# Wider instructions and another order in the pass towards the states

## The reference

```
fx = layer_norm(x, ln1_g, ln1_b)
lam_bar = exp(lam * dt);  Bu = einsum('blh,ph->blp', fx, B_bar)
xf = scan(b -> lam_bar * b + Bu);  xb = scan in the other direction
h = 2 * real(einsum('blp,hp->blh', concat(xf, xb), Cc)) + D * fx
x = gelu(h) + fx
out = (x2 @ ff_enc.T) @ ff_dec.T + x2,   x2 = layer_norm(x, ln2_g, ln2_b)
```

## Time and profile before

| | us |
|---|---|
| median of 3 runs | 10253.36 (10250.67 to 10262.34) |
| the profiled execution | 10252.34 |
| its span | 10250.5 |
| TensorE busy in the span | 9482.5 (93%) |
| DVE busy | 8275.4 (81%) |
| ACT busy | 6046.8 (59%) |
| POOL busy | 1782.1 (17%) |
| matmuls of L1414, L1342, L1335 (sq), L1374, busy | 877.0, 328.5, 236.3, 313.1 |

### The profile page before, as it was taken

The page is one execution under the profiler, slowest core; times in us unless marked ns, Lnnn a source line. Parts: engine busy times, 40 slices in busy tenths (PEclk is TensorE's granted clock), DMA queues, the critical chain, the costliest instruction groups (busy, mean ns, idle before and its releaser), DMA issues.

```text
span 10250.5 us, 187671 instructions
## 1 busy us (share of the span) xinstructions
PE 9482.5 (93%) x73254; PEld 6605.6 (64%) x73254; DVE 8275.4 (81%) x12487; ACT 6046.8 (59%) x9559; POOL 1782.1 (17%) x1824
## 2 busy tenths in 40 slices
PE   1899988999899998998989999899898999989998
PEld 1677765656577775565667777565566777656555
DVE  7788878878688887887868888787886888878786
ACT  0666654555666665454766666545476666545556
POOL 0000003333300001333320000233341000032333
PEclk9999989999999999998999999899999999989999
DMA  4667666575676766557567776646666666574655
GB/s 112 148 142 146 141 137 207 172 228 157 157 150 142 146 142 172 180 169 233 156 152 146 142 146 142 201 161 194 187 178 130 129 130 129 120 224 161 216 166 156
DMA packets 1333116, 1651.84 MB, mean 161 GB/s; under 512 B 845180, under 2 KB 1077260, under 8 KB 1246860
## 3 DMA queue, kind: packets, MB, share of 16 engines
q1 hardware_dynamic: 1332236, 1639.84, 63.7%
HBM read 786.58 MB, written 514.86 MB: 127 GB/s over the span
## 4 chain that ended last, share of the span: by engine, by line
PE 80%; DVE 10%; ACT 4%; issue 3%; DMA 1%; SPq 1%; POOL 1%; DVEq 0%; ACTq 0%; POOLq 0%
PE ps L823 14%; PE ps L1766 14%; PE ps L1779 7%; PE ps L790 6%; PE ps L1790 5%; PE ps L781 5%; PE ps L837 4%; DVE S L1546 3%; PE ps L856 3%; PE ps L881 3%; PE ps L1414 2%; PE ps L868 2%; PE ps L1335 2%; PE ps L817 2%; PE ps L884 2%
## 5 line engine op out<-in xcount | busy, mean ns | idle before, releaser
L1152 DVE SCALAR_TENSOR_TENSOR F<-U,LW,F 106x512 f32<-106x512 f32 x2048 | 1536.0, 750 | 54.5
L1766 PE MATMUL ps<-fp,Dwr 128*128 128x512 f32 x6144 | 1546.6, 401 | 0.0
L1766 PEld LDWEIGHTS ps<-fp,Dwr 128*128 128x128 f32 x6144 | 1115.6, 188 | 613.5 <-ACT x L1855 292.1
L1130 DVE TENSOR_TENSOR Z<-ps,LW 128x340 f32<-128x340 f32 x1024 | 522.7, 510 | 741.5 <-PE ps L790 721.5
L1855 ACT ACTIVATE x<-ps,cst 128x512 f32<-128x512 f32 x512 | 351.8, 687 | 1012.9 <-PE ps L1779 1009.0
L823 PE MATMUL ps<-P,WP 128*128 128x512 f32 x3072 | 905.7, 417 | 31.8 <-DMA H<-P 31.8
L823 PE MATMUL ps<-H,WP 128*128 128x512 f32 x3072 | 916.7, 420 | 0.0
L1414 PE MATMUL ps<-fp,Bwr 128*128 128x512 f32 x3072 | 877.0, 425 | 21.5 <-DVE fp L1515 21.5
L1779 PE MATMUL ps<-XP,Cwr 128*128 128x512 f32 x3072 | 802.7, 398 | 78.3 <-DVE XP L1901 78.3
L950 ACT ACTIVATE XF<-ps 128x340 f32<-128x340 f32 x1024 | 466.4, 455 | 682.3 <-PE ps L781 681.6
L1070 POOL TENSOR_SCALAR xo<-xo 64x512 f32<-64x512 f32 x4 | 6.0, 1500 | 4835.7 <-DVE xo L1186 4835.7
(11 more groups left out here) (300 smaller groups left out, 19816.7 us busy)
## 6 DMA issues: line engine op xcount, KB each, us to landing
H<-P SPq DMA_DIRECT2D x512, 585.0 KB, 7.2
raw<-x SPq DMA_DIRECT2D x240, 640.0 KB, 11.5
fx_d<-fx SPq DMA_DIRECT2D x112, 1024.0 KB, 3.9
fl_d<-fp SPq DMA_DIRECT2D x112, 1024.0 KB, 5.6
fp<-fl_d SPq DMA_DIRECT2D x112, 1024.0 KB, 6.4
fx<-fx_d SPq DMA_DIRECT2D x112, 1024.0 KB, 5.5
x1h_d<-xo SPq DMA_DIRECT2D x256, 256.0 KB, 9.0
x1v_d<-xo SPq DMA_DIRECT2D x512, 128.0 KB, 8.0
```

The costliest lines, as they stand in the source:

```text
L1130: e.tensor_tensor(Z[t % 2][:, 2 * c:2 * c + 2, :].rearrange("p a b -> p (a b)"), ps[6][:, 0:2 * HID], Wt, ALU.mult).then_inc(sem["z"], 1)
L1152: ins = e.scalar_tensor_tensor(o, u, wd[0:106, i:i + 1], o, ALU.mult, ALU.add)
L1766: ins = e.matmul(bank(m)[:], Dwr[:, w, c:c + 128], fq[n % 2][x][:, s2, :], start=(s2 == 0 and w == 0 and x == 0), stop=False)
```

## The change

Six things change in the pass towards the states:

- The broadcast of a chunk is one product of 512 columns by a summed block of `Bc`, in place of four of 128. Its operand `RD` has the deviations four times, each times a mask of 0 and 1 (`own_q`); ACT writes it with four instructions of 128 columns (`blocks`). `deviations` writes its result back to `rs`, and a semaphore `rd` stands between ACT and TensorE.
- `var` of a group runs as one row of 16 products at the end of the round, with `sq` of four chunks instead of two.
- The order in the rounds of TensorE, ACT and DVE is another: the four broadcasts together, the four norms together.
- A rotation instruction forms two products of 512 columns: bank `ps` is read twice through a broadcast, against cosine and sine. `tt` has its last two parts exchanged, which POOL's reads follow.
- `part` takes two chunks per instruction.
- `Bc` has 1024 columns in place of 2560, here and in the second pass.

```diff
-    def var(g, i):
...
+            if g:
                 e.wait_ge(sem["sd"], NG * f + g)
-            variances(e, ps[2], i, sq[:, i % 2, :], En).then_inc(sem["var"], 1)
+            for i in range(4):
+                e.wait_ge(sem["sq0"], M * f + 4 * g + i + 1)
+                variances(e, ps[2], i, sq[:, i, :], En).then_inc(sem["var"], 1)
...
             if i == 0:
-                e.wait_ge(sem["rs"], NG * f + g + 1)
+                e.wait_ge(sem["rd"], NG * f + g + 1)
...
-            spread(e, ps[3 + n % 2], i, g).then_inc(sem["bc"], 1)
+            e.matmul(ps[3 + n % 2][:], Bc[:, 128 * i:128 * i + 128], RD[:], start=True, stop=True).then_inc(sem["bc"], 1)
...
             center(g, 0)
-            bc(g - 1, 0)
-            bc(g - 1, 1)
-            var(g, 0)
             bmm(g - 2, 0)
-            var(g, 1)
+            bmm(g - 2, 1)
             center(g, 2)
-            bc(g - 1, 2)
-            bmm(g - 2, 1)
-            var(g, 2)
-            bc(g - 1, 3)
+            for i in range(4):
+                bc(g - 1, i)
             bmm(g - 2, 2)
-            var(g, 3)
             bmm(g - 2, 3)
+            var(g)
...
+        def blocks(g):
+            if g < 0:
+                return
+            e.wait_ge(sem["rs"], NG * f + g + 1)
+            if g:
+                e.wait_ge(sem["bc"], M * f + 4 * g)
+            for q in range(4):
+                ins = e.activation(RD[:, 128 * q:128 * q + 128], rs[:], ACT.Identity, scale=own_q[:, q:q + 1])
+            ins.then_inc(sem["rd"], 1)
...
-            e.tensor_tensor(piece(fp[g % 2][1], i, d), piece(fx[g % 2], i, d), piece(fp[g % 2][0], i, d).bitcast(F32),
-                            ALU.subtract).then_inc(sem["f2"], 1)
+            e.tensor_tensor(piece(fp[g % 2][1], i, d, 2), piece(fx[g % 2], i, d, 2), piece(fp[g % 2][0], i, d, 2).bitcast(F32),
+                            ALU.subtract).then_inc(sem["f2"], 2)
...
-                e.scalar_tensor_tensor(tt[:, k, :], ps[p][:], cB[:, c:c + 1], v, ALU.add, ALU.mult).then_inc(sem["t"], 1)
+            k, p, c = (0, 5 + 2 * (g % 2), 2 * d) if half else (2, 6, 2 * d + 1)
+            u = ps[p][:].unsqueeze(1).to_broadcast([128, 2, 512])
+            e.scalar_tensor_tensor(tt[:, k:k + 2, :], u, cB[:, c:c + 1], TBi[:], ALU.add, ALU.mult).then_inc(sem["t"], 2)
```

More of the change, by code:

```diff
@@ L1315, in pa_sp, with deviations @@
             lane(g)
-    def deviations(e, own, m, done, value, out):
+    def deviations(e, own, done, value, out):
         e.wait_ge(sem[done], value)
@@ L1336, in variances @@
                            start=(i == 0), stop=(i == 3))
[L1337 to L1342, removed]
         return ins
@@ L1450, in xcsq @@
             e.wait_ge(sem["ctr"], M * f + n + 1)
-            if n >= 2:
-                e.wait_ge(sem["var"], M * f + n - 1)
+            if n >= 4:
+                e.wait_ge(sem["var"], M * f + n - 3)
             u, v = [t.rearrange("p (s w j) -> p s w j", s=4, w=8) if d else t.rearrange("p (s r) -> p s r", s=4)
-                    for t in (sq[:, i % 2, :], xc[:, n % 8, :])]
+                    for t in (sq[:, i, :], xc[:, n % 8, :])]
             x = (ps[n % 2][:].rearrange("p (j s w) -> p s w j", s=4, w=8) if d else
@@ L1474, in pa_act @@
             xcsq(g, 1)
-            round_(g - 1, 0)
+            blocks(g - 1)
             xcsq(g, 2)
-            round_(g - 1, 1)
+            for i in range(4):
+                round_(g - 1, i)
             xcsq(g, 3)
-            round_(g - 1, 2)
-            round_(g - 1, 3)
             if g < NG:
@@ L1527, in rotate @@
                 e.wait_ge(sem["badd"], NG * f + g)
-            co, si = TBi[:, 0, :], TBi[:, 1, :]
-            j0 = 5 + 2 * (g % 2)
-            for k, p, v in ((0, j0, co), (3, j0, si)) if half else ((1, 6, si), (2, 6, co)):
-                c = 2 * d + (p == 6)
-                e.scalar_tensor_tensor(tt[:, k, :], ps[p][:], cB[:, c:c + 1], v, ALU.add, ALU.mult).then_inc(sem["t"], 1)
+            k, p, c = (0, 5 + 2 * (g % 2), 2 * d) if half else (2, 6, 2 * d + 1)
+            u = ps[p][:].unsqueeze(1).to_broadcast([128, 2, 512])
+            e.scalar_tensor_tensor(tt[:, k:k + 2, :], u, cB[:, c:c + 1], TBi[:], ALU.add, ALU.mult).then_inc(sem["t"], 2)
         def scan(g):
@@ L1554, in pa_dve @@
             if 0 <= g - 1 < NG:
-                deviations(e, own, g - 1, "sd", NG * f + g, "rs")
+                deviations(e, own, "sd", NG * f + g, "rs")
             rotate(g - 3, 0)
-            norm(g - 1, 0)
-            norm(g - 1, 1)
             rotate(g - 3, 1)
@@ L1562, in pa_dve @@
                 badd(e, NG - 1, 0).then_inc(sem["baddd"], 1)
+            for i in range(4):
+                norm(g - 1, i)
             part(g - 1, 0)
-            norm(g - 1, 2)
-            part(g - 1, 1)
+            part(g - 1, 2)
             scan(g - 3)
-            norm(g - 1, 3)
-            part(g - 1, 2)
-            part(g - 1, 3)
             if g == 1 and d and b + 1 < NB:
@@ L1810, in bc @@
                 e.wait_ge(sem["gl"], M * f + m + 3)
-            e.matmul(ps[3 + 2 * (m % 2)][:], Bc[:, 2048 + 128 * s:2176 + 128 * s], RD[:], start=True,
+            e.matmul(ps[3 + 2 * (m % 2)][:], Bc[:, 512 + 128 * s:640 + 128 * s], RD[:], start=True,
                      stop=True).then_inc(sem["bd"], 1)
```

32 lines of the change are left out of this document (15 added, 17 removed), and 2 rows, old and new, of the table SEMAPHORES.

## The result

The changed kernel takes 9997.11 us (median of 4 runs, 9992.64 to 9999.93), the kernel before in the same comparison 10255.32 (10250.67 to 10262.34). The ratio is 0.9747, with an interval of 0.973 to 0.9764. The sign and the kind of the change were right, two sizes in it were not.

What follows compares the result with a forecast made beforehand. DVE was taken as the nearer bound, with TensorE's loop as long after the change; 14 rounds in eight passes gaining 1.72 us gave 10252.3 - 193 + 10 - 1 = 10068, rounded to 10067 us, range 10030 to 10135.

Steps and rivals of the forecast that it cites:

- the price of the low parts beside POOL: DVE's list: two wide low parts 2.44 us, plus 0.35 us kept for the first one meeting POOL's last 0.4 us.
- the clock: TensorE's lower-clock stretches in the eight passes: four in a pass, each costing 0.3 us more, 10 us charged.
- its two waits: DVE's idle in a steady round before: 0.68 us for the third broadcast, 0.53 for ACT's rounding; both were to go.
- RD is hidden: ACT's four writings of RD before the first broadcast: 1.3 us, covered by DVE's rotations and TensorE's second centring, 0.4 left.
- The round, 11.5 forecast: Steady round of the passes towards the states: from 13.22 to 11.5 us, DVE's sum being 11.43 and TensorE's loop 11.4.
- the 1.05 row: DVE row of the earlier trace: a low part beside a running POOL instruction, 0.36 us longer than the usual 0.69.
- TensorE, 11.4 forecast: TensorE's loop in a steady round: 10.29 us of work plus 1.1 idle before the third and fourth broadcasts.
- rival (a): TensorE becomes the bound through longer broadcast waits: a round of 12.0 us, 10125 us in all; chance 0.22.
- Rival (c): Faster than forecast: POOL's stretch gone and the clock falling less often; 11.2 us a round, 10027 us; chance 0.08.
- Rival (d): Slower by TensorE's clock falling behind pieces with little array work; two a round give 14.3 us, 10340 us; chance 0.04.
- The signs of being wrong: DVE waiting for broadcasts, first broadcast waiting for ACT, pass clock well under 0.9, or second pass or convolution stage changing.
- 14 rounds at the full gain: Rounds counted as gaining 1.72 us in each of eight passes of 16 groups: 8 x 14 x 1.72 = 193 us.

Runs made afterwards that it cites:

- rd_late2: The changed kernel with two further 128-column instructions on ACT ahead of RD, result unused; 10027.17 us, ratio 0.9781.
- pool_long: The changed kernel with one more 512-column addition on POOL in each group but the last two, result unused; 10109.49 us, ratio 0.986.
- var_spread: The changed kernel with the sums of squares in four rows between the products instead of one row; 10083.1 us, ratio 0.9833.
- order_only: The kernel before with only the new order and sq of four chunks; broadcasts, rotations and low parts stay narrow; 10053.32 us, ratio 0.9809.
- rd_late: The changed kernel with four further 128-column instructions on ACT ahead of RD, result unused; 10179.39 us, ratio 0.9928.
- rot_only: The kernel before with the wide rotations and nothing else; 10246.8 us, ratio 0.9996.
- bc_only: The kernel before, in the old order, with the 512-column broadcast and ACT's writing of RD; 10674.43 us, ratio 1.0416.
- wide_norm: The changed kernel with ps3 and ps4 as one tile of two banks and two norms of 1024 columns; 10128.9 us, ratio 0.9881.
- narrow: The changed kernel with four rotations of 512 columns and four low parts of one chunk; 10034.28 us, ratio 0.9785.
- narrow_rot: The changed kernel with four rotations of 512 columns in place of two of 1024; 10022.28 us, ratio 0.9773.
- warm: The changed kernel with five further 512-column products behind the first centring in rounds 0 and 1 of each pass, result unused; 9969.49 us, ratio 0.9726.
- old_bc: The changed kernel with four 128-column broadcasts a chunk straight from the deviations, without RD; 10045.32 us, ratio 0.9796.

## Why the prediction missed

Two steps failed, each worth some 40 us: the price of the low parts beside POOL, and the clock, which was charged where it gave time back. By the profiled executions 260 us were gained where 184 were forecast. The 76 between them are these two, 39 and 41, within the rounding of the other terms.

**The loop was read rightly.** DVE's list is the bound, its two waits go, TensorE waits before the third and fourth broadcast, RD is hidden, the transfers are too. The rotations, the scan, RD and the deviations came within 0.03 us of their terms.

**The round, 11.5 forecast and 11.14 measured.** The term that failed is the low parts with POOL's stretch: 2.44 + 0.35 forecast, 2.41 measured. Of that, 0.17 is an overlap left out. A wide low part lasts 1.22 us as forecast, but the next instruction may start 0.08 us before its end; the forecast took this off for the rotations and not for the low parts. Without POOL beside it the pair costs 1649.71 - 1647.44 = 2.27 us in `rd_late2`, not 2.44. The other 0.21 us is the stretch, which I took over from the 1.05 row as a price for one meeting. `pool_long` shows that the price goes with the overlap, and the overlap was 0.26 us instead of 0.4, because the norms took 2.48 rather than 2.38 and POOL 2.52 rather than 2.6. Of the 0.10 that the norms cost more, 0.08 is DVE's short wait for the third broadcast. So the 0.07 that I added because the two loops have to meet was about right, and only stood in another place of the sum. Together -0.38 + 0.10 - 0.07 = -0.35, and times 112 rounds that is 39 us.

**TensorE, 11.4 forecast and 11.17 measured** (1644.61 - 1633.44, products to products), came near by two errors that partly cancel. Broadcasts with their waits took 2.33 us, 0.3 more than forecast: the second starts 0.34 us behind the first, not 0.23. The products took 2.84 + 2.95 = 5.79 instead of 6.32, since a product costs 0.24 us in a row of twelve and 0.26 in rows of six. I had carried over 1.58 from rows of a shape that the change abolishes. A row of twelve stood in the trace of the kernel before, in the second pass, and took 1880.28 - 1877.40 = 2.88 us:

```profile
1877.40 3.04 PE L1766 MATMUL ps<-fp,Dwr 128*128 128x512 f32 x12
```

With rows of six, and the sums between them, the kernel is `var_spread`, 11.93 us and bound by TensorE's loop, near the 12.0 of rival (a).

**The clock had the wrong sign.** I charged 10 us because the stretches at the lower clock would stay and bite harder. They went, all 27 of the steady rounds, and gave 31. That is 41 us between forecast and result. The step that failed is taking 0.97 of the earlier trace rows as fixed and pricing only its effect. Rival (c) had the round of 11.2 us and the clock falling less often, but gave the clock nothing of its own and came to 10027. `order_only` shows that the order alone ends the stretches, without the wide broadcast. `var_spread`, where DVE waits 0.82 us and no stretch stands, shows that DVE may wait. Rival (d) had the opposite sign and nothing of it came. The signs of being wrong that the prediction names are all of a slower kernel; none of them came either, and the forecast was wrong towards the fast side. The Trainium skill ("TensorE: Matmul & The Clock Gate", section "A second HAM failure mode: psum-queue depth-cycling") says that short idles between groups of matmuls can make the clock swing. The runs agree in part. The changed kernel has such idles in every round, 0.67 us and the one behind it, and no stretch, while with 0.87 us more, in `rd_late`, it swings. But `rot_only` swings more often than the kernel before, with a shorter idle.

**What stays open** is what exactly tips the clock. Stretches stand in the kernel before (one wait of 1.39 us, short broadcasts behind it; 27), `rot_only` (1.15; 34), `bc_only` (3.66; 96), `rd_late` (0.87 and 0.55; 54), `pool_long` (21) and `wide_norm` (0.21 and 1.47; 13). None stand in the steady rounds of `narrow` (where TensorE waits 1.00 us for the first norm), `narrow_rot`, `rd_late2`, `warm`, `old_bc` and the order alone, whose broadcasts are as short as before, nor in `var_spread`. So short broadcasts alone do not bring them, and a wait of 1.00 us alone does not. In the changed kernel more wait in one round does, but across the kernels the number of stretches does not follow the size of the wait. No rule finer than this was separated.

**The count.** 14 rounds at the full gain stood for 12 steady rounds, first rounds and drain. Measured outside the steady rounds are 12 + 15 + 4 = 31 us against the 27.5 of two rounds a pass: about right.

## What to carry to other kernels

Read both lists of a loop for who waits on whom, then try the order first: here it gave 197 of 258 us without saving an instruction, and one of the edits of the same change was worth 425 us in the other direction without it. Price a matmul or a vector instruction from a row with the same neighbours as after the change, and price two engines that take turns by their overlap, not by a stretch seen once. Where the granted clock falls in the steady part, put a figure on it going away as well as on its staying, and count the stretches before and after a change: in `rot_only` a real gain in the quiet rounds was lost to more of them.

## What the runs showed of the hardware

- An addition on POOL and a DVE subtraction with both inputs in SBUF take turns: POOL's 1.30 us became 2.26 beside a low part, and the pair of low parts 3.31 to 3.57 instead of 2.35. In four places the DVE instruction was longer by the overlap less some 0.14 us. Norms, with one input from PSUM, were not stretched.
- Twelve products of 512 columns in a row took 2.84 to 2.95 us, two rows of six behind another kind 3.18.
- A rotation that reads one bank twice through a broadcast lasted 1.28 us for 1024 columns, no more than plain columns cost by the 1.04 ns of the earlier trace rows.
- DMA engines 92% busy with one queue put no wait on DVE in these rounds.
- The lower clock in steady rounds came and went with small changes of TensorE's waits: with the changed kernel's order none at 0.28 us ahead of the broadcasts, 54 of 96 rounds at 0.87. In the old order a wait of 1.39 us went with 27 and one of 1.15 with 34.
